# Loading the expert indexes of the first four tiles together, and turning half of the indicators before v is ready, in a one-core Flamingo block

## The chip, the cores and the metric

The kernel runs on one core of a Trainium2 chip. The metric is the device time of one execution in microseconds (us), as the median of several runs. Engines: TensorE (PE; PEld is its weight load), VectorE (DVE), ScalarE (ACT), GpSimd (POOL) and SyncE (SP), which only issues DMAs. Each engine runs its own instructions in the order in which they are written; semaphores tie the engines together.

## The reference

16 batches of 256 tokens with 512 features pass through cross attention and then a mixture of 8 experts, of which each token takes 2.

```python
x = x + tanh(g_xattn[0]) * xattn(layernorm(x), ctx, Wq, Wkv)
x = x + tanh(g_ffn[0]) * ffn(layernorm(x), ...)

def ffn(x, ...):
    probs = softmax(einsum('bsd,de->bse', x, gate_w) + gate_b, axis=1)   # over the tokens of a batch
    vals, idx = top_k(probs, 2)
    h = relu(x @ w1[e] + b1[e]); h = relu(h @ w2[e] + b2[e]); y = relu(h @ w3[e] + b3[e])
    v = einsum('ebso,bse->eo', y, w_tok)      # one row per expert, summed over ALL tokens
    out = einsum('bse,eo->bso', ind, v)       # ind[b,s,e] = 1 where the token takes expert e
```

So the experts' outputs are not given back to their tokens: they are summed into v (8 x 512), and each token adds the two rows of v of its experts.

## The kernel before, in words

Products are made in three passes of split fp32 numbers (hi x hi, hi x lo, lo x hi; lines 1446 to 1448), so nearly every operand has a hi part made by ScalarE and a lo part made by VectorE or GpSimd.

**Attention, batches 0 to 15** (to some 324 us). Each batch is attended, normalised to xn2, sent to DRAM (`xn2_dram`) and gated. The slot of each token in its expert's list is worked out on VectorE (`slots`, lines 1070 to 1094), and GpSimd writes (token, weight) pairs to that slot of `slot_pair` in DRAM with four indirect DMAs per batch (`send_pairs`, line 678). The list of the first 8 tiles is made after 12 batches (`early_table`).

**Expert tiles.** A tile is 352 slots of one expert; tile 0 starts while the last batches are still in work. For a tile m SyncE loads its 352 indexes (`load_idx`, line 535: three DMAs of 128, 128 and 96 pairs, behind a read of the table), GpSimd gathers those rows of xn2 from DRAM into `xg` (`gather`, line 708: three indirect DMAs), and TensorE turns them (`row_transposes`, line 1723). ScalarE and VectorE make et_hi (line 924) and et_lo from the result, TensorE runs layers 1 to 3, and VectorE adds the weighted sum into `v_sum`. From tile 4 on the turning is done by DMAs and VectorE. There is one `idx` and one `xg` buffer: `load_idx(m)` waits for gather m - 1 (semaphore `gathered`), and `gather(m)` waits for index m (`idx_in`) and for `te_done` of tile m - 1.

**Where attention and experts meet,** the order on each engine is written out by hand. On GpSimd: the last batch's part of the loop, `gather(1)`, `send_pairs(13)`, `norm2_scale(15)`, `gather(2)`, `send_pairs(14)`, and so on (lines 728 to 739). `norm2_scale(15)` (lines 645 to 664, output rn) gives the scale with which ScalarE makes xn2 of batch 15 (`norm2`, line 828, xn in the profile); behind it ScalarE has `et_high(1)`, `split_w(0, 1)` (w_hi, line 885) and `gt_high(15)`. VectorE follows with `et_low(1)`, slots(14), `w_low` and `gt_low(15)`. TensorE has the first product of layer 2 of tile 0 (lines 1669 to 1671), `ranks(14)` (line 1517), `xn2_transposes(15)` (line 1460), which waits for xn2 and for the second piece of et_low(1) (its PSUM bank), then the second half of layer 2 and `gate_logits(15)` (line 1565), which waits for gt_low(15). SyncE's order there stands in lines 546 to 568.

**The tail.** After the last tile VectorE makes v in bf16 parts (`v3`, lines 1420 to 1427). TensorE turns the indicators `ind_all` of two batches at a time (`turn_indicators(k)`, k = 0 to 7, four matmuls each, line 1782) into two PSUM banks in turn, and ScalarE copies them to `ind24` (`indicators(k)`, line 973). TensorE turns v (line 1790), VectorE and ScalarE copy it (lines 1429 and 979), and then 32 rows of products follow (line 1803), one per 128 tokens, in 6 banks. VectorE adds 26 of them to x (line 1436), GpSimd 6 (rows 11, 15, ... 31, copied by ScalarE; line 752). SyncE sends a batch of output when its two rows are there (line 619). Groups 2 to 7 of the indicators stand on TensorE ahead of rows 2, 6, 10, 14, 18 and 22.

Of the kernel before, what the change touches and what calls it, by code (L numbers as in the profile page):

```python
# [9 lines left out]
U32 = mybir.dt.uint32  # L10
# [72 lines left out]
EARLY = 8  # L83

# [38 lines left out]
def flamingo_block(nc, x, x_t, ctx_t, g_xattn, g_ffn, wq_t, wk_t, wv, gate_w, gate_b,  # L123
# [15 lines left out]
    with ExitStack() as ctx:  # L139
# [32 lines left out]
        v_sum = alloc(ctx, "v_sum", [P, E, DC], F32)  # L172
        ind_all = alloc(ctx, "ind_all", [P, B, RC, 3, E], BF16)
# [209 lines left out]
        tail_small, wsum_step, part_done = sem("tail_small"), sem("wsum_step"), sem("part_done")  # L383
        v_step, vt_done, v24_ready = sem("v_step"), sem("vt_done"), sem("v24_ready")
# [18 lines left out]
        turn_banks = [bank[2], bank[3]]  # L403
# [32 lines left out]
        def _(sp):  # L436
# [93 lines left out]
            def load_idx(m):  # L530
                need(sp, gathered, 16 * TH * m)
                wait_alone(sp, "sp")
                r = sp.value_load(table[0:1, bass.ds(m, 1), 1:2], min_val=0, max_val=NSLOT - TILE)
                for c, (first, rows) in enumerate(CHUNKS):
                    sp.dma_start(idx[0:rows, c], slot_pair[bass.ds(r + first, rows)]).then_inc(idx_in, 16)
# [13 lines left out]
            load_idx(0)  # L549
# [5 lines left out]
            load_idx(1)  # L555
# [5 lines left out]
            load_idx(2)  # L561
# [6 lines left out]
            load_idx(3)  # L568
# [55 lines left out]
        def _(pool):  # L624
# [70 lines left out]
            def gather(m):  # L695

                need(pool, idx_in, 16 * TH * (m + 1))
# [9 lines left out]
                for c, (_, n) in enumerate(CHUNKS):  # L707
                    pool.indirect_dma_start(xg[0:n, c], None, rows,  # L708
                                            bass.IndirectOffsetOnAxis(ap=idx[0:n, c, 0:1], axis=0)
# [46 lines left out]
        def _(act):  # L756
# [214 lines left out]
            def indicators(k):  # L971
                act.wait_ge(turned, k + 1)
                act.activation(ind24[:, 2 * k * S:2 * (k + 1) * S], turn_banks[k % 2][0:3 * E], ACT.Copy
                               ).then_inc(ind24_done, 1)

            indicators(0)
            indicators(1)
            act.wait_ge(vt_done, 1)
            act.activation(v24[:, D // 2:], bank[1][0:3 * E, 0:D // 2], ACT.Copy).then_inc(v24_ready, 1)
            for n in range(B * RC):  # L980
                if n % 4 == 2 and n // 4 + 2 < PAIRS:
                    indicators(n // 4 + 2)
# [457 lines left out]
        def _(pe):  # L1440
# [335 lines left out]
            def turn_indicators(k):  # L1776
                if k >= 2:
                    pe.wait_ge(ind24_done, k - 1)
                for i in range(2 * RC):
                    rows = ind_all[:, 2 * k + i // RC, i % RC].rearrange("p r e -> p (r e)")  # L1780
                    out = turn_banks[k % 2][0:3 * E, i * P:(i + 1) * P]
# [4 lines left out]
            turn_indicators(0)  # L1786
            turn_indicators(1)
            pe.wait_ge(v_step, 1 + 4)
            for c in range(DC):
                last = pe.matmul(bank[c // 2][0:3 * E, (c % 2) * P:(c % 2 + 1) * P],  # L1790
                                 v3[:, c].rearrange("p r e -> p (r e)"), ident_half[:], start=True, stop=True)
            last.then_inc(vt_done, 1)
            pe.wait_ge(v24_ready, 2)
            for n in range(B * RC):
                if n % 4 == 0:
                    pe.wait_ge(ind24_done, n // 4 + 1)
                if n % 4 == 2 and n // 4 + 2 < PAIRS:
                    turn_indicators(n // 4 + 2)
# [49 lines left out]
```

## Time and profile before

| | |
|---|---|
| median of 3 runs | 922.4 us (921.86 to 922.59) |
| the profiled execution | 923.1 us |
| its span | 921.3 us |
| mean granted clock of TensorE | 0.984 of full speed |
| TensorE busy | 903.1 us, 98% |
| VectorE busy | 710.8 us, 77% |
| ScalarE busy | 506.5 us, 55% |
| GpSimd busy | 284.1 us, 31% |
| DMA | 144.97 MB, mean 157 GB/s |

Times are in us from the start of the span. The span is the profiled execution as the profiler sees it; the execution's own time holds 1.8 us more around it. The clock is given as a share of 2.4 GHz; it has two levels, 1.2 and 2.4 GHz, and a value between them is a mix of both. Matmuls are pipelined: a matmul's start to the start of the next one tells its cost, not its duration. In a timeline the number in square brackets is how long the engine had been idle before the row, and what ended that. An "x3" row holds three instructions without a pause. Releasers are inferred from the last semaphore event before the start.

### The profile page before, as it was taken

The numbers are of one execution on the slowest core, as the hardware profiler recorded it, in microseconds if no ns is written. First come the engines' busy times: TensorE is split into PE (matmuls) and PEld (weight loads), VectorE is DVE, ScalarE is ACT, GpSimd is POOL, SyncE is SP. The second block draws the span as 40 slices with busy tenths as digits, with TensorE's granted clock in tenths as the row PEclk, the third lists the DMA queues.
The fourth block names the chain that finished last, engine by engine and source line by source line (L and its number), as shares of the span: only waits on it lengthen the run. The fifth ranks groups of instructions, "written<-read, shape, count | busy, mean of one in ns | idle before, by whom it ended". The sixth has DMA issues, their size and how long they took to land.

```text
span 921.3 us, 18692 instructions
## 1 busy us (share of the span) xinstructions
PE 903.1 (98%) x5650; PEld 850.8 (92%) x5650; DVE 710.8 (77%) x1305; ACT 506.5 (55%) x703; POOL 284.1 (31%) x314
## 2 busy tenths in 40 slices
PE   9999999999999989999999999999999999999985
PEld 6989888898888889999999999999999999999971
DVE  6667888888888877868777777777777777777665
ACT  5355444554445566556666666666666666666432
POOL 4234555554554458712111111111111111110003
PEclk9999999999999999999999999999999999999995
DMA  7434543345432745377757888853753753751008
GB/s 241 161 122 146 156 149 114 114 161 167 127 92 72 166 125 139 95 172 226 201 156 201 247 245 247 246 157 110 201 156 110 201 156 110 201 156 49 17 31 351
DMA packets 105412, 144.97 MB, mean 157 GB/s; under 512 B 29728, under 2 KB 70432, under 8 KB 102176
## 3 DMA queue, kind: packets, MB, share of 16 engines
q1 hardware_dynamic: 97952, 127.15, 46.2%
q0 software_dynamic: 7424, 17.38, 7.2%
q8 instruction: 18, 0.29, 0.1%
q14 instruction: 18, 0.15, 0.1%
HBM read 112.95 MB, written 31.53 MB: 157 GB/s over the span
## 4 chain that ended last, share of the span: by engine, by line
PE 90%; POOL 2%; issue 2%; DMA 2%; DVE 1%; SPq 1%; ACT 1%; POOLq 0%; DVEq 0%; ACTq 0%
PE bank L1446 28%; PE bank L1448 27%; PE bank L1447 27%; PE bank L1803 1%; POOL slot_pair L678 1%; DMA idx<-slot_pair 1%; PE bank L1567 1%; PE bank L1524 1%; PE bank L1569 0%; PE bank L1586 0%; DMA wk_raw<-in_wk_t 0%; PE bank L1460 0%; PE bank L1480 0%; PE bank L1723 0%; PE bank L1782 0%
## 5 line engine op out<-in xcount | busy, mean ns | idle before, releaser
L1446 PE MATMUL bank<-h_hi,w_hi 128*128 128x352 f32 x744 | 242.2, 326 | 0.0
L1448 PE MATMUL bank<-h_hi,w_lo 128*128 128x352 f32 x744 | 240.7, 324 | 0.0
L1447 PE MATMUL bank<-h_lo,w_hi 128*128 128x352 f32 x744 | 239.7, 322 | 0.0
L708 POOL DMA_INDIRECT xg<-xn_dram,idx x72 | 86.1, 1196 | 367.6 <-DMA idx<-slot_pair 351.9
L1023 DVE TENSOR_TENSOR w_lo<-w_raw,w_hi 128x2048 fp32r<-128x2048 f32 (+1 forms) x74 | 166.6, 2251 | 23.6 <-ACT w_hi L885 18.6
L902 ACT ACTIVATE h<-bank,bias 128x352 f32<-128x352 f32 x192 | 95.9, 551 | 138.3 <-PE bank L1448 137.8
L885 ACT ACTIVATE w_hi<-w_raw 128x2048 fp32r<-128x2048 f32 x71 | 135.5, 1908 | 35.4 <-PE bank L1448 32.0
L1023 DVE TENSOR_TENSOR h_lo<-h,h_hi 128x704 fp32r<-128x704 f32 x88 | 78.1, 888 | 83.0 <-ACT h_hi L908 83.0
L1446 PEld LDWEIGHTS bank<-h_hi,w_hi 128*128 128x128 f32 x744 | 140.5, 189 | 0.0
L1447 PEld LDWEIGHTS bank<-h_lo,w_hi 128*128 128x128 f32 x744 | 140.4, 189 | 0.0
L1448 PEld LDWEIGHTS bank<-h_hi,w_lo 128*128 128x128 f32 x744 | 139.9, 188 | 0.0
L1446 PE MATMUL bank<-et_hi,w_hi 128*128 128x352 f32 x376 | 121.5, 323 | 0.0
L1447 PE MATMUL bank<-et_lo,w_hi 128*128 128x352 f32 x376 | 120.5, 321 | 0.0
L1448 PE MATMUL bank<-et_hi,w_lo 128*128 128x352 f32 x376 | 120.5, 320 | 0.0
L678 POOL DMA_INDIRECT slot_pair<-pair,slot_u x64 | 68.8, 1075 | 68.2 <-DVE pair L1094 47.4
L908 ACT ACTIVATE h_hi<-h 128x704 fp32r<-128x704 f32 x96 | 76.3, 794 | 6.5 <-PE bank L1569 2.7
L1447 PEld LDWEIGHTS bank<-et_lo,w_hi 128*128 128x128 f32 x376 | 70.7, 188 | 0.0
L1446 PEld LDWEIGHTS bank<-et_hi,w_hi 128*128 128x128 f32 x376 | 70.6, 188 | 0.0
L1448 PEld LDWEIGHTS bank<-et_hi,w_lo 128*128 128x128 f32 x376 | 70.5, 188 | 0.0
L1446 PE MATMUL bank<-xt_hi,a_hi 128*128 128x256 f32 x240 | 69.2, 288 | 0.0
L1447 PE MATMUL bank<-xt_lo,a_hi 128*128 128x256 f32 x240 | 67.9, 283 | 0.0
L1448 PE MATMUL bank<-xt_hi,a_lo 128*128 128x256 f32 x240 | 67.9, 283 | 0.0
(222 smaller groups left out, 1740.7 us busy)
## 6 DMA issues: line engine op xcount, KB each, us to landing
w_raw<-in_w SPq DMA_DIRECT2D x24, 1024.0 KB, 5.7
xq<-rows_dram SPq DMA_DIRECT2D x80, 176.0 KB
w_raw<-in_w SPq DMA_DIRECT2D x48, 256.0 KB, 6.9
rows_dram<-xg SPq DMA_DIRECT2D x20, 512.0 KB, 3.3
wb<-slot_pair SPq DMA_DIRECT2D x24, 352.0 KB, 4.4
xt_raw<-in_x_t SPq DMA_DIRECT2D x16, 512.0 KB, 3.8
c_raw<-in_ctx_t SPq DMA_DIRECT2D x16, 512.0 KB, 3.8
x_all<-in_x SPq DMA_DIRECT2D x16, 512.0 KB, 4.8
```

The costliest lines, as they stand in the source:

```text
L678: pool.indirect_dma_start(slot_pair, bass.IndirectOffsetOnAxis(ap=slot_u[:, k, n:n + 1], axis=0), pair[:, k, n], None).then_inc(pair_sent[ ...
L708: pool.indirect_dma_start(xg[0:n, c], None, rows, bass.IndirectOffsetOnAxis(ap=idx[0:n, c, 0:1], axis=0)).then_inc(gathered, 16)
L885: act.activation(w_hi[n][:], w_raw[n][:], ACT.Copy).then_inc(w_his[n], 1)
L902: act.activation(h[:, oc], layer_banks(n, m)[oc][:, 0:TILE], ACT.Relu, bias=bias[n][:, oc:oc + 1]).then_inc(relu_done[n], 1)
L908: act.activation(h_hi[n][:, 2 * k:2 * k + 2], h[:, 2 * k:2 * k + 2], ACT.Copy).then_inc(h_his[n], 1)
L1023: dve.tensor_tensor(dst, src, hi.bitcast(F32), ALU.subtract).then_inc(done, 1)
L1446: pe.matmul(out_ap, lh, rh, start=(i == 0), stop=False)
L1447: pe.matmul(out_ap, lh, rl, start=False, stop=False)
L1448: last = pe.matmul(out_ap, ll, rh, start=False, stop=(i == n - 1))
L1524: last = pe.transpose(bS[:, k * S + c * P:k * S + (c + 1) * P], pexp[:, c, k * P:(k + 1) * P], ident[:])
L1567: pe.matmul(R_LOGIT, gw[:, i, 0:E], gt_lo[:, i], start=False, stop=False)
L1803: pe.matmul(out_banks[n % 6][:], ind24[:, n * P:(n + 1) * P], v24[:], start=True, stop=True).then_inc(o_done, 1)
```

## The change

Indexes: tiles 0 to 3 get an index buffer and a semaphore each (`first_idx`, `first_idx_in`). SyncE loads all four ahead of the first weights, without waiting for a gather; the loads of 1, 2 and 3 go from their old places. Tile 4 uses `idx` first, without a wait for a gather. `gather(m)` waits for the buffer's own semaphore.

Indicators: four PSUM banks hold groups 0 to 3, all turned at the start of the tail; v's transposes then wait for two of ScalarE's copies, since they use banks 0 and 1. Group 4 is turned behind v's transposes, groups 5, 6 and 7 ahead of rows 2, 6 and 10. ScalarE copies groups 4 to 7 in the places of rows 0, 2, 4 and 6.

```diff
+IDX_EARLY = 4
...
+        first_idx = [alloc(ctx, f"first_idx{n}", [P, TH, 2], U32) for n in range(IDX_EARLY)]
...
-        turn_banks = [bank[2], bank[3]]
+        turn_banks = [bank[n] for n in (0, 1, 2, 3, 2, 3, 2, 3)]
...
             def load_idx(m):
-                need(sp, gathered, 16 * TH * m)
-                wait_alone(sp, "sp")
+                if isinstance(m, int) and m < IDX_EARLY:
+                    into, done = first_idx[m], first_idx_in[m]
+                else:
+                    into, done = idx, idx_in
+                    if not (isinstance(m, int) and m == IDX_EARLY):
+                        need(sp, gathered, 16 * TH * m)
+                        wait_alone(sp, "sp")
...
-            load_idx(0)
+            for m in range(IDX_EARLY):
+                load_idx(m)
             sp.wait_ge(qa_done, 2 * B)
             load_w(0, 0)
             load_w(1, 0)
             for n in range(3):
                 load_b(n, 0)
-            load_idx(1)
             store_xn2(B - 2)
...
-            load_idx(2)
...
-            load_idx(3)
...
             def gather(m):
-                need(pool, idx_in, 16 * TH * (m + 1))
+                if isinstance(m, int) and m < IDX_EARLY:
+                    rows_of = first_idx[m]
+                    pool.wait_ge(first_idx_in[m], 16 * TH)
+                else:
+                    rows_of = idx
+                    need(pool, idx_in, 16 * TH * (m - IDX_EARLY + 1))
...
-            indicators(0)
-            indicators(1)
+            for k in range(4):
+                indicators(k)
...
             for n in range(B * RC):
-                if n % 4 == 2 and n // 4 + 2 < PAIRS:
-                    indicators(n // 4 + 2)
+                if n % 2 == 0 and n // 2 + 4 < PAIRS:
+                    indicators(n // 2 + 4)
...
             def turn_indicators(k):
-                if k >= 2:
+                if k >= 4:
                     pe.wait_ge(ind24_done, k - 1)
...
-            turn_indicators(0)
-            turn_indicators(1)
+            for k in range(4):
+                turn_indicators(k)
             pe.wait_ge(v_step, 1 + 4)
+            pe.wait_ge(ind24_done, 2)
...
             last.then_inc(vt_done, 1)
+            turn_indicators(4)
             pe.wait_ge(v24_ready, 2)
...
-                if n % 4 == 2 and n // 4 + 2 < PAIRS:
-                    turn_indicators(n // 4 + 2)
+                if n in (2, 6, 10):
+                    turn_indicators(5 + n // 4)
```

SyncE, from the last index DMA of tile 0 to the first weights, before (L533 and L498 read the table, L508 loads weights):

```order
L535 DMA idx<-slot_pair 96x2
L498 TENSOR_LOAD table
L498 ISA x2
L508 ISA
L508 DMA w_raw<-in_w 32x4x512
```

and with the change, from the last index DMA of tile 2 on (line numbers of the changed kernel, L502 and L512 being the lines of the weights):

```order
L544 DMA first_idx<-slot_pair 96x2
L542 TENSOR_LOAD table
L542 ISA x2
L544 ISA
L544 DMA first_idx<-slot_pair 128x2
L544 ISA
L544 DMA first_idx<-slot_pair 128x2
L544 ISA
L544 DMA first_idx<-slot_pair 96x2
L502 TENSOR_LOAD table
L502 ISA x2
L512 ISA
```

Three such index loads, each with its read of the table, now stand ahead of the first weights.

TensorE in the tail, from the first indicators to the third row, before:

```order
L1782 MATMUL bank<-ident_half,ind_all 24x128 [waits slot_step]
L1782 MATMUL bank<-ident_half,ind_all 24x128 x7
L1790 MATMUL bank<-ident_half,v 24x128 [waits v_step]
L1790 MATMUL bank<-ident_half,v 24x128 x3
L1803 MATMUL bank<-v,ind 128x512 [waits ind24_done,v24_ready]
L1803 MATMUL bank<-v,ind 128x512
L1782 MATMUL bank<-ident_half,ind_all 24x128 [waits ind24_done]
```

and with the change:

```order
L1794 MATMUL bank<-ident_half,ind_all 24x128 [waits slot_step]
L1794 MATMUL bank<-ident_half,ind_all 24x128 x15
L1804 MATMUL bank<-ident_half,v 24x128 [waits ind24_done,v_step]
L1804 MATMUL bank<-ident_half,v 24x128 x3
L1794 MATMUL bank<-ident_half,ind_all 24x128 [waits ind24_done]
L1794 MATMUL bank<-ident_half,ind_all 24x128 x3
L1818 MATMUL bank<-v,ind 128x512 [waits ind24_done,v24_ready]
L1818 MATMUL bank<-v,ind 128x512
L1794 MATMUL bank<-ident_half,ind_all 24x128 [waits ind24_done]
```

Eight more matmuls stand ahead of the transposes of v, four between these and the first row, and v's transposes wait for ScalarE as well.

## Rows read from the trace of the kernel before

**Rows 1.** Waits of TensorE, whole span: engine, line, releaser, us in total, times, longest

```profile
PE bank L1460 <- DVE et_lo L1023: 3.3, 1, 3.3
PE bank L1790 <- DVE v L1427: 2.1, 1, 2.1
```

**Rows 2.** Timeline of TensorE, 319 to 349 us: start, us, engine, line, what, idle before

```profile
319.87 1.58 PE L1723 MATMUL bank<-ident,xg 128*128 128x128 f32 x12
...
334.85 0.41 PE L1669 MATMUL bank<-h_hi,w_hi 128*128 128x352 f32 x1
...
338.75 0.18 PE L1517 MATMUL bank<-ind,tri_half 128*128 128x16 bf16 x1
...
342.22 1.45 PE L1460 MATMUL bank<-ident,xn 128*128 128x128 f32 x8 [3.25 <-DVE et_lo L1023]
343.32 0.64 PE L1446 MATMUL bank<-h_hi,w_hi 128*128 128x352 f32 x1
...
348.64 0.28 PE L1565 MATMUL bank<-gt_hi,gw 128*40 128x256 f32 x1
```

**Rows 3.** Window 340:345: length, busy PE, PEld, DVE, ACT, POOL, PEclk, DMA share, GB/s

```profile
340.00:345.00 5.00, 2.78 (x14) 2.81 (x15) 4.08 (x13) 5.00 (x8) 2.70 (x4) 0.80 0.73 187
```

**Rows 4.** Timeline of GpSimd, 316 to 348 us

```profile
327.23 1.10 POOL L708 DMA_INDIRECT xg<-xn_dram,idx  x1 [10.90 <-DMA idx<-slot_pair]
...
335.79 1.10 POOL L678 DMA_INDIRECT slot_pair<-pair,slot_u  x1 [0.31 <-issue]
...
338.52 0.20 POOL L664 TENSOR_TENSOR rn<-rn 128x2 f32<-128x2 f32 x1
...
347.14 3.07 POOL L678 DMA_INDIRECT slot_pair<-pair,slot_u  x1 [0.30 <-issue]
```

**Rows 5.** Timeline of SyncE's DMA issues, 300 to 315 us

```profile
300.26 1.43 SPq L535 DMA_DIRECT2D idx<-slot_pair  x3
306.30 2.99 SPq L508 DMA_DIRECT2D w_raw<-in_w  x4
...
311.31 2.64 SPq L527 DMA_DIRECT2D bias<-in_b  x3
314.79 1.39 SPq L535 DMA_DIRECT2D idx<-slot_pair  x3
```

**Rows 6.** Timeline of ScalarE, 327 to 342 us

```profile
327.12 1.89 ACT L885 ACTIVATE w_hi<-w_raw 128x2048 fp32r<-128x2048 f32 x1
...
333.30 1.00 ACT L902 ACTIVATE h<-bank,bias 128x352 f32<-128x352 f32 x2 [2.35 <-PE bank L1448]
...
338.75 1.52 ACT L828 ACTIVATE xn<-x_all,rn 128x512 f32<-128x512 f32 x2 [3.63 <-POOL rn L664]
...
341.50 1.91 ACT L885 ACTIVATE w_hi<-w_raw 128x2048 fp32r<-128x2048 f32 x1
```

**Rows 7.** Timeline of VectorE, 331 to 346 us

```profile
331.35 0.25 DVE L1020 BATCH_NORM_AGGREGATE mv<-st 128x2 f32<-128x6 f32 x2
...
340.78 1.75 DVE L1023 TENSOR_TENSOR et_lo<-bank,et_hi 128x512 fp32r<-128x512 f32 x3 [3.60 <-ACT et_hi L924]
...
345.87 1.28 DVE L1023 TENSOR_TENSOR gt_lo<-bank,gt_hi 128x512 fp32r<-128x512 f32 x2
```

**Rows 8.** DMA issues of 310 to 311 us, the last number being us to landing

```profile
w_raw<-in_w SPq DMA_DIRECT2D x1, 1024.0 KB, 13.7
```

**Rows 9.** Timeline of TensorE, VectorE and GpSimd in the tail

```profile
894.03 0.39 PE L1790 MATMUL bank<-ident_half,v 128*24 128x128 bf16 x4 [2.09 <-DVE v L1427]
894.46 0.41 DVE L1429 CAST v<-bank 24x256 bf16<-24x256 f32 x1 [0.48 <-PE bank L1790]
...
902.10 1.29 POOL L752 TENSOR_TENSOR x_all<-v_rows,x_all 128x512 f32<-128x512 f32 x1 [90.15 <-ACT v_rows L986]
```

**Rows 10.** Two windows of the tail, columns as in rows 3

```profile
904.00:905.00 1.00, 1.00 (x6) 0.33 (x4) 0.84 (x3) 0.37 (x1) 0.55 (x1) 0.50 0.73 291
915.00:916.00 1.00, 0.00 (x0) 0.00 (x0) 0.00 (x0) 0.00 (x0) 0.00 (x0) 0.50 1.00 397
```

More of the change, by code:

```diff
@@ L383, in flamingo_block @@
         tail_small, wsum_step, part_done = sem("tail_small"), sem("wsum_step"), sem("part_done")
+        first_idx_in = [sem(f"first_idx_in{n}") for n in range(IDX_EARLY)]
         v_step, vt_done, v24_ready = sem("v_step"), sem("vt_done"), sem("v24_ready")
@@ L530, in load_idx @@
             def load_idx(m):
-                need(sp, gathered, 16 * TH * m)
-                wait_alone(sp, "sp")
+                if isinstance(m, int) and m < IDX_EARLY:
[5 more added lines that the diff above has]
+                        wait_alone(sp, "sp")
                 r = sp.value_load(table[0:1, bass.ds(m, 1), 1:2], min_val=0, max_val=NSLOT - TILE)
                 for c, (first, rows) in enumerate(CHUNKS):
-                    sp.dma_start(idx[0:rows, c], slot_pair[bass.ds(r + first, rows)]).then_inc(idx_in, 16)
+                    sp.dma_start(into[0:rows, c], slot_pair[bass.ds(r + first, rows)]).then_inc(done, 16)
             def load_wb(m):
@@ L708, in gather @@
                     pool.indirect_dma_start(xg[0:n, c], None, rows,
-                                            bass.IndirectOffsetOnAxis(ap=idx[0:n, c, 0:1], axis=0)
+                                            bass.IndirectOffsetOnAxis(ap=rows_of[0:n, c, 0:1], axis=0)
                                             ).then_inc(gathered, 16)
@@ L972, in indicators @@
                 act.wait_ge(turned, k + 1)
-                act.activation(ind24[:, 2 * k * S:2 * (k + 1) * S], turn_banks[k % 2][0:3 * E], ACT.Copy
+                act.activation(ind24[:, 2 * k * S:2 * (k + 1) * S], turn_banks[k][0:3 * E], ACT.Copy
                                ).then_inc(ind24_done, 1)
-            indicators(0)
-            indicators(1)
+            for k in range(4):
+                indicators(k)
             act.wait_ge(vt_done, 1)
@@ L1780, in turn_indicators @@
                     rows = ind_all[:, 2 * k + i // RC, i % RC].rearrange("p r e -> p (r e)")
-                    out = turn_banks[k % 2][0:3 * E, i * P:(i + 1) * P]
+                    out = turn_banks[k][0:3 * E, i * P:(i + 1) * P]
                     last = pe.matmul(out, rows, ident_half[:], start=True, stop=True)
```

## The prediction, written before the changed kernel ran

> **What bounds the kernel now.** I read the waits of TensorE first, then its own timeline, then the chain that released the one wait inside the work, and the tail last. The waits come first because TensorE is busy for 98% of the span (the table above): an edit can pay only where TensorE stands still or is slow, or behind its last product. There are two waits worth naming [rows 1]: 3.3 us before the transposes of the last batch's rows (line 1460), put down to VectorE's et_lo, and 2.1 us before v is transposed (line 1790).
>
> The first one costs more than its 3.25 us [rows 2]. The 24 products of tile 0's second half of layer 2 run from 343.32 to 348.64, 5.32 us. The 24 before the wait, of the same 352 columns, run from 334.85 to 338.75, 3.90 us. The difference of 1.42 us is the clock: 0.80 was granted on average in 340 to 345 us [rows 3], so a part at 1.2 GHz behind the wait, where the stretch before had 2.4 GHz. The place costs 3.25 + 1.42 = 4.67 us.
>
> Who made TensorE wait? Follow it back. GpSimd begins gather(1) at 327.23, after 10.90 us idle for an index DMA [rows 4]. Behind it, in its own order, stand the four sends of batch 13 (the last ends at 336.89) and the small operations that give batch 15's norm its scale (the last ends at 338.72). ScalarE waits 3.63 us for that scale and starts xn at 338.75; et_hi and VectorE's et_lo follow, and TensorE starts at 342.22. The index itself was asked for at 314.79, behind 2 MB of weights and three biases in SyncE's queue [rows 5], while the index of tile 0, asked for at 300.26, met an empty queue. So the index of tile 1 was late by its place in the queue, not by its size.
>
> **The index part of the change.** It moves the index loads of tiles 1, 2 and 3 directly behind that of tile 0, each into a buffer of its own, so none of them needs the gather before it. GpSimd's gather(1) then waits only for the buffer xg, free when TensorE's transposes of tile 0 end (319.87 + 1.58 = 321.45 [rows 2]). I take 321.6 for its start, 5.6 us earlier. The seven DMA issues of gather(1) and the sends took 336.89 - 327.23 = 9.66 us [rows 4], so they end at 331.3. The scale needs batch 15's statistics as well, and the small operations took 338.72 - 336.89 = 1.83 us. ScalarE is free from 338.75 - 3.63 = 335.12 [rows 6], and the statistics end at 331.60 [rows 7]. The scale is there at 331.6 + 1.8 = 333.4, so the late one is now **ScalarE itself, at 335.1**, 3.65 us earlier than before, with 1.7 us to spare for GpSimd. Nothing on ScalarE or VectorE between xn and et_lo waits for anything else, so the piece of et_lo that released TensorE at 342.22 now does so at 338.57. TensorE is ready at 342.22 - 3.25 = 338.97. The wait goes, by a margin of 0.4 us.
>
> What is late next? The gate's logits at 348.64 need gt_lo of batch 15, which ended at 347.15 [rows 7]. It comes behind et_lo and ScalarE's w_hi of 341.50 without a pause, so it moves by the same 3.65, to 343.50. TensorE gets there at 338.97 + 1.10 (the transposes, 342.22 to 343.32) + 3.90 = 343.97. That is 0.5 us of margin; I price it at nothing. From there ScalarE waits for TensorE again, so the later work moves with TensorE.
>
> What the move delays: SyncE issues three more index loads ahead of the weights. One takes 314.79 + 1.39 - 313.95 = 2.23 us with its read of the table [rows 5], so the first weights are issued at about 301.69 + 3 x 2.23 + 0.84 = 309.2 instead of 306.30, 2.9 us later. The weights of layer 2 were issued between 310 and 311 and landed 13.7 us later [rows 8], at 323.7 to 324.7; with all of the delay at 326.6 to 327.6. ScalarE wants them at 327.12 [rows 6]. At worst 0.5 us late, and ScalarE has 2.35 us idle before 333.30 to make it good. At the lower end they are not late at all: gather(0) has the DMA engines to itself meanwhile and is out of the way when the weights come. Cost on the path: 0 between both bounds. The queue's later items (bias, xn2 stores, wb) lose an index load each ahead of them. Load 4 no longer waits for gather(3), but gather(4) is four tiles away from being late: nothing.
>
> **The tail part.** Sixteen indicator transposes instead of eight run while VectorE makes v. TensorE idled 2.09 us there [rows 9], and eight more at some 0.1 us each (0.39 for four of the same kind) take 0.8 of it. The fifth group is issued behind the transposes of v, while VectorE copies v for 0.41 us: 0.39 beside 0.41, nothing. The new wait for two copies of ScalarE ends before v is made. The first output row starts where it did. Between rows, three groups of four fewer stand on TensorE, 3 x 0.39 = 1.2 us. I give none of it to the sum: after all engines were done, in 915 to 916 us, the DMA engines still had a share of 1.00 and moved 397 GB/s [rows 10]. The outputs are 16 x 512 KB = 8.39 MB, 21 us at that rate, more than the 20 us from the end of the copy of v (894.87) to a time at which no engine works any more, so **the output queue sets the end**, and it starts with batch 0, which does not move. What can be won is the hole of 904 to 905, where the share was 0.73, some 0.3 us: there batch 5 waited for GpSimd's first row (902.10 to 903.39 [rows 9]). The groups between rows ahead of that row are as many as before, so I expect it to stay. Bounds of this part: 0 to -0.3, and +0.1 if the fifth group outlasts the copy.
>
> **Sum.** -3.25 - 1.42 + 0 = -4.67 us. Of the profiled execution, 923.1 becomes 918.4 and its span 921.3 becomes 916.6. The median of the runs, 922.4, is 0.7 below that execution; the same -4.67 on it gives **917.7 us**.
>
> **Rivals.**
> (A) *GpSimd's issues grow slow.* gather(1) moves under VectorE's weight subtractions, and one issue of this kind took 3.07 us at 347.14 instead of 1.1 [rows 4]. One such is 2.0 us, against 1.7 of margin; two are 4.0, and xn then starts at 337.4, TensorE at 340.9. Of the 3.25 us, 1.3 are won and the clock may fall all the same: gain 1.3 to 2.8, time 919.6 to 921.1. For it: such issues are in the trace. Against: 9.66 us already hold issues beside VectorE.
> (B) *The tail's clock stays up.* In 904 to 905 us TensorE was busy all the time at a granted 0.50, 1.2 GHz. The idle ahead of the rows shrinks from 2.1 to 1.3 us; if that keeps the 2.4 GHz, GpSimd's first row comes earlier and the hole closes: 917.4. Against: ten us into the rows a TensorE without a pause still had not got its clock back. The Trainium skill, "TensorE: Matmul & The Clock Gate", under "What's actually happening", has sustained activity release the throttle; by that rule rows in succession would run at full clock. This trace does not agree for rows of 24 partitions.
> (C) *The weights become the wait* (slower). If nine small transfers hold up the queue for more than their issues, layer 2's weights come late. From their landing, w_hi 1.89, relu 1.00 [rows 6] and two splits of 704 columns have to pass before TensorE's 334.85. I estimate the splits from the w_hi row (2048 columns in 1.89) and the gt_lo row (1024 in 1.28) at 0.7 + 0.9. So landings up to 330.3 cost nothing, some 6 us later than before, and only 10.7 us later is the gain eaten. At 14 us the time is 922.4 + 3.3 = 925.7. Against: the queue is empty when they go out, and 2.9 us is all that their issues take.
> (D) *The change does not free gather(1)*, because another wait stands behind the index: 922.4. Against: te_done is 5.8 us older than the start, and the buffer is free.
>
> **Chances.** Forecast 0.70; A 0.13; B 0.10; C 0.04; D 0.03. A measurement of this kernel tells about 0.2%, 1.8 us, from no change. Faster: forecast, B and most of A, 0.91. Within: D and the slowest of A, 0.05. Slower: C, 0.04. The range runs from 916.7 (B, and 0.7 us between runs as 921.86 to 922.59 shows) to 919.9 (the better end of A), which leaves out some 0.15.
>
> **What would show it.** Right: gather(1) starts at about 321.6 with no wait for an index; xn begins at 335.1 with no wait for rn; no idle before the transposes of line 1460's last call; the granted clock is 1.00 in 340 to 345; tile 0's 24 products take 3.9 us. The tail from the transposes of v to the end of the span keeps its 921.3 - 894.03 = 27.3 us, with a DMA share near 1.00 to the end. Wrong: xn still waits for rn (A); w_hi of layer 2 waits for a DMA (C); the tail is shorter by more than 0.3 us, so that production and not the output queue bounds it.

## The result, and the profile after

| | before | changed |
|---|---|---|
| median, first measurement (3 runs each) | 922.4 us (921.86 to 922.59) | 916.73 us (916.5 to 917.42) |
| ratio to before | | 0.9938 [0.9925, 0.9952] |
| ratio, measured again (7 runs, 27 of before) | | 0.9961 [0.9946, 0.9976] |
| ratio, a third time (6 runs, 17 of before) | | 0.9956 [0.9944, 0.9968] |
| profiled execution, its span | 923.1, 921.3 us | 916.73, 914.5 us |
| mean granted clock | 0.984 | 0.988 |

The changed kernel is faster, as forecast, but 5.7 us faster in the first measurement where 4.7 was forecast. Two more measurements, with more runs, gave 3.6 and 4.1 us (1 - 0.9961 and 1 - 0.9956 of 921.6; the medians themselves lie 3.6 and 3.0 us apart). The forecast lies between these three figures, and for a wrong reason, as the experiments show: one term of its sum was too large, and another, which was put at nothing, was worth 1.1 to 1.7 us.

The waits of TensorE in the changed kernel, columns as in [rows 1]:

```profile
PE bank L1804 <- DVE v L1439: 1.6, 1, 1.6
PE bank L1482 <- POOL zeros L632: 1.2, 1, 1.2
PE bank L1472 <- ACT xn L840: 0.9, 2, 0.6
```

The 3.3 us of [rows 1] ahead of batch 15's transposes are gone (line 1472 is the old 1460; none of its 0.9 lies ahead of batch 15's transposes, where the timeline below shows no idle time), and the wait for v has shrunk from 2.1 to 1.6. GpSimd's timeline, as [rows 4]:

```profile
322.61 1.10 POOL L720 DMA_INDIRECT xg<-xn_dram,first_idx  x1 [5.97 <-issue]
...
331.01 0.97 POOL L685 DMA_INDIRECT slot_pair<-pair,slot_u  x1 [0.30 <-issue]
332.07 0.97 POOL L652 TENSOR_SCALAR rn<-mv 128x2 f32<-128x2 f32 x1
333.12 1.22 POOL L654 TENSOR_TENSOR rn<-rn,mhalf 128x2 f32<-128x2 f32 x1
334.54 0.43 POOL L669 TENSOR_SCALAR rn<-mv 128x2 f32<-128x2 f32 x1 [0.20 <-POOL rn L654]
335.06 0.20 POOL L671 TENSOR_TENSOR rn<-rn 128x2 f32<-128x2 f32 x1
```

gather(1) waits for no index. It begins at 322.61, 4.6 us earlier than in [rows 4], not the 5.6 forecast (tile 0's transposes ended at 321.76, and 0.85 us lie between that and the gather's start, where the forecast had 0.15), and the small operations behind the sends took 3.2 us instead of 1.8. The scale was ready at 335.26 and not at 333.4. ScalarE, which answers to [rows 6]:

```profile
334.64 0.79 ACT L920 ACTIVATE h_hi<-h 128x704 fp32r<-128x704 f32 x1
335.34 1.51 ACT L840 ACTIVATE xn<-x_all,rn 128x512 f32<-128x512 f32 x2
```

xn begins without a wait, at 335.34 (forecast 335.1). The 1.7 us that GpSimd was to have in hand had gone to almost nothing. TensorE, the last operation ahead of the transposes, these, and what follows, as in [rows 2]:

```profile
338.73 0.17 PE L1530 MATMUL bank<-ind,ones_half 128*128 128x16 bf16 x1
338.83 1.21 PE L1472 MATMUL bank<-ident,xn 128*128 128x128 f32 x8
339.79 0.41 PE L1458 MATMUL bank<-h_hi,w_hi 128*128 128x352 f32 x1
...
343.82 0.31 PE L1577 MATMUL bank<-gt_hi,gw 128*40 128x256 f32 x1
```

```profile
340.00:345.00 5.00, 5.00 (x35) 4.61 (x34) 4.96 (x8) 3.66 (x6) 3.47 (x2) 1.00 0.58 198
```

No idle time, the clock at 1.00 in the window of [rows 3], and the gate's product at 343.82 instead of 348.64: 4.8 us. At v's transposes it is 894.03 - 889.37 = 4.66 us, the 4.67 of the sum. But the spans differ by 6.8, so another 2.1 us were won in the tail. SyncE, to compare with [rows 5], had the weights out at 310.40 (forecast 309.2), and no w_hi waited for them:

```profile
300.42 9.10 SPq L544 DMA_DIRECT2D first_idx<-slot_pair  x12
310.40 2.98 SPq L512 DMA_DIRECT2D w_raw<-in_w  x4
```

The tail of the changed kernel: v's transposes, GpSimd's first and last row, as in [rows 9], then a window, as in [rows 10]:

```profile
889.37 0.39 PE L1804 MATMUL bank<-ident_half,v 128*24 128x128 bf16 x4 [1.65 <-DVE v L1439]
...
896.52 1.27 POOL L764 TENSOR_TENSOR x_all<-v_rows,x_all 128x512 f32<-128x512 f32 x1 [89.26 <-ACT v_rows L998]
...
905.46 1.28 POOL L764 TENSOR_TENSOR x_all<-v_rows,x_all 128x512 f32<-128x512 f32 x1 [0.52 <-ACT v_rows L998]
```

```profile
900.00:901.00 1.00, 1.00 (x3) 0.10 (x1) 1.00 (x3) 0.00 (x1) 0.92 (x1) 0.50 0.99 393
```

GpSimd's first row comes 7.15 us behind v's transposes, 8.07 before, and the hole in the transfers is gone in this execution. What ended the tail was not plain yet.

### The profile page after: what moved, and what is told of

It reads as the page before. It is cut to its first block, busy times and chain, and to the rows that moved or that the text cites. A ratio compares the mean times of both kernels' runs of the same rounds, so it can differ in the third digit from the quotient of the medians.

```text
span 914.5 us, 18688 instructions
## 1 busy us (share of the span) xinstructions
PE 899.8 (98%) x5650; PEld 848.2 (93%) x5650; DVE 711.4 (78%) x1305; ACT 506.3 (55%) x703; POOL 286.9 (31%) x314
## 4 chain that ended last, share of the span: by engine, by line
PE 94%; POOL 1%; DVE 1%; issue 1%; ACT 0%; DMA 0%; POOLq 0%; SPq 0%; DVEq 0%
PE bank L1458 29%; PE bank L1459 28%; PE bank L1460 28%; PE bank L1818 1%; POOL slot_pair L685 1%; PE bank L1579 1%; PE bank L1536 1%; PE bank L1735 1%; PE bank L1581 1%; PE bank L1598 1%; PE bank L1472 0%; DMA wk_raw<-in_wk_t 0%; PE bank L1492 0%; PE bank L1493 0%; PE bank L1487 0%
## 5 line engine op out<-in xcount | busy, mean ns | idle before, releaser
L720 POOL DMA_INDIRECT xg<-xn_dram,idx x60 | 72.2, 1203 | 352.8 <-DMA idx<-slot_pair 340.5
```

Of the source, the lines that this page charges most:

```text
L720: pool.indirect_dma_start(xg[0:n, c], None, rows, bass.IndirectOffsetOnAxis(ap=rows_of[0:n, c, 0:1], axis=0)).then_inc(gathered, 16)
```

## The experiments

The later runs form four groups, each on one chip with the kernel before beside the others (its median 921.5, 921.6, 921.2 and 921.6 us); a ratio is always to the kernel before of the same group. Microseconds of gain are worked out from the ratios; the differences of the medians lie up to 1.1 us from them. For the profiles I cut the span at two places that every kernel has: A, from the first product of layer 2 of tile 0 to v's transposes (boundary and expert tiles), and T, from there to the end (tail). Before: A 894.03 - 334.85 = 559.2, T 27.3. Changed: 554.6 and 25.1.

### The two parts alone

The index part alone (the change without its indicator part), twice; the second time beside the whole change:

> The index part of the change alone, on the tail of before. Theory 1 (the wait of 3.25 us and the slow clock behind it are worth 4.7 us, and the tail gave about 1.0 of the 5.7): this gains 4.7, ratio 0.9949. Theory 2 (all of the gain comes from the index part, the tail is bound by the output queue and gives nothing): 5.7, ratio 0.9938.

> The index part alone, again, now beside the whole change. If the profile that was late from its start-up (first weights 1.2 us late) was an accident: v's transposes begin at 889.5 to 890.5, as in the whole change. Theory that the parts add: 1 to 2 us above the whole change and 1 to 2 us below before. Rival that the index part is all of it: the same as the whole change within 0.3 us.

The indicator part alone, also twice:

> The indicator part alone, with the index loads of before. Theory 1: it gains 1.0 us, ratio 0.9989; in the trace the clock falls later after the first row, GpSimd's first row comes earlier and the hole in the output queue is closed. Theory 2: 0 (-0.3 to +0.1), ratio 1.000. The profile tells whether the last DMA engine still runs 1.2 us longer than the others, as it did in the profile of before.

> The indicator part alone, again. Theory that the parts add: 1 to 2 us above the whole change, 1 to 2 us below before. Theory that the boundary's wait is worth 4.7 us by itself: 4.5 us above the whole change and the same as before. In its profile the wait of TensorE ahead of the transposes of xn2 of batch 15 should be there again, 1.5 to 3.3 us.

The whole change again:

> The changed kernel again, beside the two parts alone and before. Theory (the first comparison is the kernels' own): 4 to 6 us below before, both parts' gains adding (the parts alone measured -1.0 and -1.7 us against before on another occasion, which would leave 1 to 3 us that only the pair gives). Rival (the profiled execution of before at the first measurement was one of its longer ones: wait of 3.3 us and a fall of the clock at the boundary, and a DMA engine that ran on alone at the end): 2.5 to 3.5 us below before, the sum of the parts. Its profile: no wait ahead of the transposes of xn2 of batch 15, clock 1.00 between 335 and 350, v's transposes to the end 25.0 to 25.5.

Measured in the group of these three: index part 0.9980 [0.9968, 0.9992], indicator part 0.9982 [0.9971, 0.9994], both 0.9961 [0.9946, 0.9976]. The first time the parts alone gave 0.9987 [0.9976, 0.9998] and 0.9988 [0.9976, 0.9999]. So **the parts add**, within intervals of some 0.12% to either side: 0.20% and 0.18% against 0.39%. The indicator part, priced at nothing, is worth about as much as the index part, priced at everything. The rival of the last expectation, that the first profile of before was a long one, fits best (2.5 to 3.5 us there, 3.6 measured).

In the profiles of the index part A was 554.6 both times and T 26.7 and 27.5, the old tail. In those of the indicator part A was 558.3 and 556.0, T 26.3 and 25.2. Waits of TensorE with the indicator part alone (its first profile):

```profile
PE bank L1460 <- DVE et_lo L1023: 1.5, 1, 1.5
...
PE bank L1669 <- DVE h_lo L1023: 1.1, 1, 1.1
```

The boundary's wait is back, half as long as in [rows 1], with another of 1.1 us ahead of it, and the granted clock in 340 to 345 stayed at 1.00.

### What the boundary costs

Filler on TensorE in the kernel before, ahead of the transposes that waited:

```diff
             ranks(B - 2)
+            for n in range(48):
+                pe.matmul(bank[2][:, 0:P], ident_half[:], ones_half[:], start=True, stop=True)
             xn2_transposes(B - 1)
```

> Before with 48 matmuls of 128 columns on constants, written to a free bank ahead of the transposes that wait. They take some 2.7 us and end before the wait does, so the wait's end does not move. If the 1.42 us behind the wait are the clock that fell while TensorE stood idle, the clock stays at 1.00 in 340 to 345 us and the gain is 1.4 us, ratio 0.9985. If they are something else (the products waiting for data), 0.

Measured: 1.0017 [1.0005, 1.0029], 1.6 us slower, A 558.6. The filler did not do what was meant. It ran from 340.00 to 342.84, and the transposes followed at 343.04; in the indicator part's profile they began 1.44 us behind the start of VectorE's et_lo, which here would be 341.7 (et_lo began at 340.23). So the filler ended behind the wait and held TensorE some 1.4 us by itself. The clock stayed at 1.00, but it did so in most profiles with the old boundary (below), so this run does not price the clock.

The scale of batch 15 ahead of the sends of batch 13 on GpSimd, in the kernel before:

```diff
             gather(1)
-            send_pairs(B - 3, (B - 3) % 2)
             norm2_scale(B - 1)
+            send_pairs(B - 3, (B - 3) % 2)
```

> Before with one edit in GpSimd's order: the scale of batch 15 is made ahead of the four sends of batch 13. gather(1) stays as late as before, 327.2 us. If the chain to TensorE's wait is gather(1), sends, scale, xn, et_lo, as predicted, the scale is there by 333.6, xn starts at 335.1 when ScalarE is free, and the gain is that of the index part, 4.7 us. If gather(1)'s data, not the scale, is what counts, nothing is gained.

Measured: 1.0049 [1.0029, 1.0068], slower. TensorE's waits:

```profile
PE bank L1446 <- ACT h L902: 2.9, 1, 2.9
...
PE bank L1723 <- DMA xg<-xn_dram,idx: 2.0, 1, 2.0
```

The wait at line 1460 is gone, as meant, and two others took its place behind it: at 355.6 TensorE had waited 2.0 us for the rows of gather(2), which began at 342.20 instead of 339.33, and at 360.2 it had waited 2.9 us for ScalarE's h; the granted clock was 0.50 from 358 to 364. Moving the wait's last link alone makes the kernel slower. The expectation had gather(1) at 327.2 in this kernel; it came at 325.39.

The kernel before once more:

> The kernel before, profiled a second time. The stretch from layer 2 of tile 0 to v's transposes took 559.2 us in its first profile, and 556.1 to 558.3 in three kernels with the same boundary. Theory (a part of the boundary's wait, and the fall of the clock behind it, come in some executions only): 556 to 558.5 us, no fall of the clock or a shorter wait than 3.3 us. Rival (they belong to this kernel): 559 us, wait 3.3 us, clock at 1.2 GHz behind it. In both, GpSimd's last row plus its 8.6 us of drain ends the program, 27.3 us behind v's transposes.

Its second profile had A 554.8, as short as with the change, T 26.9, and no wait for et_lo at all. GpSimd's gather(1) and TensorE:

```profile
323.97 1.10 POOL L708 DMA_INDIRECT xg<-xn_dram,idx  x1 [6.84 <-DMA idx<-slot_pair]
```

```profile
340.07 1.21 PE L1460 MATMUL bank<-ident,xn 128*128 128x128 f32 x8
```

The first theory's signs are there, no fall of the clock and no wait, but A lies below its 556 to 558.5: the same instructions in the same order, and gather(1), released by the index, came 3.3 us earlier although the index was asked for 2.2 us later (316.98, against 314.79 in [rows 5]). Median of the timed runs: 921.25, ratio 0.9995 [0.9984, 1.0007], as it should be.

The four own buffers, but the loads of the indexes 1, 2 and 3 at their old places:

```diff
-            for m in range(IDX_EARLY):
+            for m in range(1):
                 load_idx(m)
...
                 load_b(n, 0)
+            load_idx(1)
...
             load_w(0, 1)
+            load_idx(2)
...
             load_w(0, 2)
+            load_idx(3)
```

> The changed kernel, with the four buffers of its own, but the indexes of tiles 1, 2 and 3 loaded at their old places, behind the weights and biases. Theory (what held the second gather was the place in the queue, behind 3 MB of weights, and not the one shared buffer): that gather waits for its index to about 327 us again, and the stretch from layer 2 of tile 0 to v's transposes takes 556 to 559 us instead of 554.6; the time is 1.5 to 2 us above the changed kernel in this call. Rival (the shared buffer's wait for the first gather was it): the gather at 322.6 us, 554.6 us, and the time of the changed kernel.

Its gather(1), ScalarE's second pair of h (layer 1 of tile 0) and xn, and two waits of TensorE:

```profile
325.94 2.13 POOL L723 DMA_INDIRECT xg<-xn_dram,first_idx  x1 [8.32 <-DMA first_idx<-slot_pair]
```

```profile
336.29 1.00 ACT L917 ACTIVATE h<-bank,bias 128x352 f32<-128x352 f32 x2 [3.95 <-remote]
...
339.15 1.52 ACT L843 ACTIVATE xn<-x_all,rn 128x512 f32<-128x512 f32 x2 [1.04 <-POOL rn L674]
```

```profile
PE bank L1475 <- DVE et_lo L1038: 1.2, 1, 1.2
PE bank L1684 <- DVE h_lo L1038: 1.2, 1, 1.2
```

A was 557.5. gather(1) waits for its index although no buffer is shared any more, so the place in the queue (behind 2 MB of weights; the 3 MB of the expectation is a slip) is enough to make the index late. The time was 0.9961 [0.9945, 0.9976] against 0.9956 [0.9944, 0.9968] for the changed kernel, 0.3 us, where 1.5 to 2 were expected: six runs each neither show that cost nor exclude it.

Of the two waits only the one for et_lo hangs on gather(1) by the chain of the prediction (sends, rn, xn, et_lo). The one for h_lo hangs on ScalarE's h, which had been idle for 3.95 us where the profile of before shows 2.35, and was released by what the profile calls "remote". **A second path of the boundary** shows here that the prediction did not have. This idle time was 3.8 to 5.1 us in five of the eight profiles with the index loads at their old places (indicator part twice, filler, old places, and the kernel with VectorE's rows, below), and 1.8 to 2.4 in the other three and in all ten with an early index. (For the second of the indicator part the profile names TensorE's product as the releaser, as before.) In two of the five (the second of the indicator part, and VectorE's rows) xn did not wait for rn at all: their loss is that of h alone. What makes h late, and whether the late index has a part in it, no run shows.

Only tiles 0 and 1 ahead of the weights, the other two behind the biases:

```diff
-            for m in range(IDX_EARLY):
+            for m in range(2):
                 load_idx(m)
...
             store_xn2(B - 2)
+            load_idx(2)
+            load_idx(3)
```

> The changed kernel, but only the indexes of tiles 0 and 1 are loaded ahead of the first weights; those of tiles 2 and 3 follow behind the biases. Theory (the index part gives its gain through the second gather alone, and gives 0.7 to 0.9 us back before the boundary, since the first product of layer 2 of tile 0 began at 335.9 us in eight traces with early indexes and at 335.0 in five without, because the weights are issued 3 to 4 us later): 0.4 to 0.9 us faster than the changed kernel in this call, layer 2 of tile 0 at 335.0 and v's transposes 554.6 us behind it, as in the changed kernel. Rival (the later weights cost nothing and the 0.9 us is chance): the same within 0.3 us.

> The changed kernel, for comparison with the three others on one chip: 3.2 to 4.2 us below before, 554.6 us from layer 2 of tile 0 to v's transposes.

Measured 0.9957 [0.9945, 0.997] and 0.9956 [0.9944, 0.9968]: the same. The weights went out at 306.57 instead of 309.57 and layer 2 began at 334.9 instead of 335.9, but in the second profile of before it began at 336.0 as well, and in the first of the changed kernel, with its weights at 310.40, at 334.8: that difference is not the weights'. The early indexes of tiles 2 and 3 add nothing that can be measured, so the index part lies in that of tile 1, and the later weights cost nothing that can be measured, as forecast.

gather(1)'s start and A, all profiles with the old boundary and neither the filler nor the norm first: 323.97 and 554.8 (before, second), 324.94 and 558.3 (indicator part), 325.65 and 556.0 (the same again), 325.94 and 557.5 (old places), 326.42 and 558.3 (the kernel with VectorE's rows, below), 327.23 and 559.2 (before, first). With the early index: 554.5 to 554.7 in ten profiles. The six average 557.4, 2.8 us above; the timed runs, which are many more, put the index part at 1.2 and 1.8 us. The first profile of before, on which the forecast stands, was the extreme of the six. The clock fell behind the boundary in two of them: there, and in the kernel with VectorE's rows, where one wait of 2.1 us for h_lo stood alone and the window 340 to 345 had 0.66. Where TensorE stood 1.0 to 1.5 us at a time it stayed at 1.00.

### What ends the tail

The output a row earlier, on top of the change (batch 0 as two DMAs):

```diff
-            for b in range(B):
+            for n in range(RC):
+                sp.wait_ge(res_dve, dve_rows(n + 1))
+                sp.dma_start(out_v[0][:, n], x_all[:, 0, n]).then_inc(out_sent, 16)
+            for b in range(1, B):
```

> The changed kernel with batch 0 of the output sent as two DMAs, one for each row, so that the first transfer begins a row earlier. Theory (the output queue moves at 400 GB/s without a pause from its first transfer to its last and sets the end): 0.3 to 0.6 us faster than the whole change in this call, since the first row is ready about 0.6 us ahead of the second. Rival (the rows' production or the last landing sets the end): within 0.1 us of it.

Measured 0.9963 [0.995, 0.9977] beside 0.9961 for the change: nothing. In its profile the first transfer did go out earlier, but the queue then stood idle for longer (its share was 0.78 in 895 to 896 and 0.55 in 900 to 901), so the first transfer alone does not set the end. That sent me to the last instructions of the program. The rows of the line that closes it, in the profile of the index part alone (old tail, second profile; columns: line, queue, what, count, ns min/median/max, start):

```profile
L141 POOLq DRAIN  x1: 8585/8585/8585, 908.7 to 908.7; - x1
L141 SPq DRAIN  x1: 7/7/7, 915.4 to 915.4; - x1
```

**GpSimd's drain takes 8.6 us.** It begins with GpSimd's last row (908.77, 1.26 us long), so it ends 7.3 us behind it: at 917.33. SyncE had seen its last output land at 915.26, the span ends at 917.55. In this execution GpSimd's last row ends the program and the output queue has 2 us in hand. The same rows of the changed kernel (first profile):

```profile
L141 POOLq DRAIN  x1: 8602/8602/8602, 905.4 to 905.4; - x1
L141 SPq DRAIN  x1: 7/7/7, 914.3 to 914.3; - x1
```

Here GpSimd is through at 905.4 + 8.6 = 914.0 and SyncE at 914.3: the two stand level. And of the kernel before:

```profile
L139 POOLq DRAIN  x1: 8585/8585/8585, 912.5 to 912.5; - x1
L139 SPq COMPARE_BRANCH  x1: 38/38/38, 920.5 to 920.5; - x1
```

912.5 + 8.6 = 921.1, 0.2 before the end of its span. In this execution the output was late as well (a few packets still ran at 29 GB/s in 919 to 920), which is why both looked level. So it was in the second profile of before:

```profile
L139 POOLq DRAIN  x1: 8618/8618/8618, 908.8 to 908.8; - x1
L139 SPq DRAIN  x1: 13/13/13, 917.1 to 917.1; - x1
```

Counted from v's transposes in all profiles, GpSimd is through at 26.4 to 28.1 us in the six with the old tail and at 24.6 to 25.4 in the eight with the new one. The last output lands at 24.8 to 26.5 and at 24.7 to 26.1: **the landing did not move with the change, GpSimd did**. In the old tail GpSimd was the later of the two each time (by 0.5 to 2.1 us), in the new one the output was later, or level within 0.2 us. (SyncE's closing branch, COMPARE_BRANCH, is taken for the landing.) The landings spread over 1.8 us for the same transfers; in some profiles a few packets ran on by themselves at the end, as above, and why is not shown.

What delays GpSimd's last row is seen in the chain that ended last. Old tail, index part alone, second profile (start, us, engine, line; L1794 are turned indicators, L1815 rows):

```profile
896.11 0.53 PE bank L1794 x4
896.64 1.81 PE bank L1815 x4
...
903.68 2.68 PE bank L1815 x6
906.39 0.61 ACT v_rows L998
907.07 1.26 POOL x_all L764
908.74 1.30 POOLq L141
```

and in the changed kernel:

```profile
894.32 0.53 PE bank L1794 x4
894.85 8.12 PE bank L1818 x18
902.99 0.60 ACT v_rows L998
903.67 1.27 POOL x_all L764
904.94 0.48 issue
905.42 1.31 POOLq L141
```

Every group of indicators between rows is 0.53 us at 1.2 GHz (0.33 at 2.4) of a chain that ends with GpSimd. Six stand between rows in the old tail and three with the change; at the price of 0.53 there are five and one in these two profiles. GpSimd's drain begins 16.0 us behind v's transposes instead of 18.6, but not all of these 2.6 us are the order's: the clock fell 3.0 us behind v's transposes here and 1.7 in the other. In the second profile of the changed kernel it fell at 1.7 as well, and there the drain begins at 16.7. So the order is worth 1.9 us at the same clock, 3 x 0.53 = 1.6 of it the three groups, and the later fall another 0.7. Then the theory was tested from both sides. GpSimd's rows to VectorE, in the kernel before:

```diff
         def by_pool(n):
-            return n >= 8 and n % 4 == 3
+            return False
```

> The kernel before, but VectorE adds all 32 rows of the tail, so that GpSimd (and its drain of 8.6 us, which in every trace so far begins at GpSimd's last row) has nothing there. New theory of the tail: in the kernel before, GpSimd's last row plus its drain ends the program, 1.9 us behind the last landing of the output; in the changed one the two end together. Expected: 1.5 to 2.2 us faster than before, v's transposes to the end 25.1 to 25.5 instead of 27.3, and the last landing to the end 0.4 instead of 2.3. Theory of the prediction (the output queue sets the end): 0 to 0.4 us faster. Rival (VectorE at 0.6 us a row is too slow alone): 0.5 us or more slower.

Two more additions behind GpSimd's last row, in the changed kernel:

```diff
             for n in filter(by_pool, range(B * RC)):
...
+            for n in range(2):
+                pool.tensor_tensor(pool_pad[:, n], v_rows[:, 1], v_rows[:, 1], ALU.add)
```

> The changed kernel with two more additions of 1.3 us each on GpSimd behind its last row, into a buffer that nobody reads. New theory (GpSimd's last work plus 8.6 us of drain is a floor of the end, and stands level with the output's last landing): 2.1 to 2.6 us slower than the changed kernel, v's transposes to the end about 27.7, drain again 8.6 us long. Theory that the output queue sets the end: no difference, since the last row is added over 5 us before the last landing.

The kernel with the two additions, its GpSimd and its closing rows:

```profile
906.52 1.29 POOL L765 TENSOR_TENSOR x_all<-v_rows,x_all 128x512 f32<-128x512 f32 x1 [0.52 <-ACT v_rows L1001]
907.76 2.04 POOL L767 TENSOR_TENSOR pool_pad<-v_rows 128x512 f32<-128x512 f32 x2
```

```profile
L141 POOLq DRAIN  x1: 10583/10583/10583, 906.5 to 906.5; - x1
L141 SPq COMPARE_BRANCH  x1: 38/38/38, 915.2 to 915.2; - x1
```

The output had landed at 915.2, and the program went on to 917.3. The drain was 10.6 us long, not 8.6 as I expected: it holds the work still queued, here 1.3 + 2.0 us, and again 7.3 behind it. T was 26.9, the time 0.9985 [0.9974, 0.9995] against 0.9961 and 0.9956 without the additions in other groups, 2.2 and 2.7 us slower (expected 2.1 to 2.6, although the two additions took 1.0 each and not 1.3). The changed kernel did not run in this group; beside the two kernels of the group without GpSimd's rows (below) it is 0.8 and 1.1 us slower. **Shown** by the trace: work on GpSimd that nobody reads, done 5 us before the last output landed, holds the end of the program 2 us behind that landing. That it costs about its own length in the median rests on the comparison between groups.

The kernel before with all rows on VectorE had T 25.8 (expected 25.1 to 25.5), and its closing rows are

```profile
L139 POOLq DRAIN  x1: 10820/10820/10820, 807.7 to 807.7; - x1
L139 SPq DRAIN  x1: 13/13/13, 918.8 to 918.8; - x1
```

with the drain 100 us before the end and the span's end at 919.1, 0.4 behind the last landing. The time was 0.9987 [0.9975, 0.9999], 1.2 us, under the 1.5 to 2.2 expected (the medians differ by 0.7 only): what lies outside the span was at least 2.1 us in its runs and at least 1.7 in those of before, so some of it came back behind the last instruction. Why, I did not find.

The same on top of the change, alone and with the two DMAs for batch 0:

> The same in the changed kernel. New theory: GpSimd's drain and the output queue end within 0.4 us of each other there, so only the hole in the transfers goes: 0.1 to 0.6 us faster than the changed kernel (918.0 in the last call), and 1.5 to 4 us faster than the previous kernel of this call, which is what the index part is worth by itself once the tails are the same. Rival (the indicators' place matters in another way than by GpSimd's last row): the difference of these two kernels is over 4 us.

> The changed kernel with all rows by VectorE and the first batch of the output sent as two DMAs of a row each. The last call's kernel with the two DMAs alone gained nothing, since the queue then ran dry for longer ahead of GpSimd's first row. Theory: with no such row there, the earlier start is kept, 0.3 to 0.7 us faster than the kernel without it in this call. Rival (a pair of rows takes about as long to make as to send, so the queue runs dry again): within 0.2 us.

Measured 0.9971 [0.996, 0.9982] and 0.9966 [0.9954, 0.9977]. Against the 0.9961 and 0.9956 of the changed kernel in other groups these are no gain; the 0.1 to 0.6 us expected of the first did not come, and the two DMAs on top, for which 0.3 to 0.7 were expected, are not separated from it (0.05%). The first is 1.5 us faster than the kernel before with the same rows on VectorE (0.9971 against 0.9987, same group), at the lower end of the 1.5 to 4 expected for the index part with the tails alike. The first had T 25.1 (the changed kernel 25.1 to 26.5), the second 26.5: in both GpSimd was out of the way and only the output queue was left. No version that I ran beats the changed kernel by what can be measured.

Mean of T: old order of the indicators with GpSimd's rows, five profiles (before twice, index part twice, filler), 27.1 us (the kernel with the norm first had 28.3; its clock fell before v's transposes); new order, eight profiles with GpSimd's six rows and nothing behind them, 25.6. The difference, 1.5 us, fits the 1.1 and 1.7 us of the indicator part alone.

## Why the prediction was right and wrong

- **"The index of tile 1 was late by its place in the queue."** Right; own buffers at the old places left gather(1) at 325.94 with 8.32 us of waiting. How late is another matter (third point).
- **The chain from gather(1) to TensorE, and its arithmetic.** Right in its links: no wait for rn, none for et_lo, clock 1.00, 24 products in 4.0 us, and 4.66 us won at v's transposes for 4.67 forecast. But gather(1) came 1.0 us later than forecast and GpSimd's small operations took 1.4 us longer. The margin of 1.7 us was all but used up; a little more and rival A would have held. And the boundary has a second path, ScalarE's late h, which made TensorE wait 1.0 to 2.1 us in five profiles and is not in the prediction at all.
- **"The place costs 3.25 + 1.42 = 4.67 us."** One of the two steps that failed, by its size: it is the sum's only term, and the runs put the part at 1.2 and 1.8 us. It was read from one execution, and the place is not a constant. By A it cost 4.6 us there, 0.2 in the second profile of the same kernel, where the index landed earlier for no reason that a run shows, and 1.4 to 3.7 in the four others. The fall of the clock that made up 1.42 of it appeared in two of six profiles with the old boundary.
- **The later weights at nothing.** Right in what can be seen: w_hi waited for no DMA, and the kernel with the weights 3.0 us earlier took the same time. Rival C did not appear.
- **"The output queue sets the end", and with it the tail at 0 with bounds of 0 to -0.3.** Wrong, and this is the other step that failed, by its mechanism: the part measured 1.1 and 1.7 us alone, and 2.1 in the first pair of profiles. The window of 915 to 916 us in [rows 10] showed busy DMA engines and idle compute engines, and I took what is busy last for what ends last. The old tail ended with GpSimd's drain, 0.5 to 2.1 us behind the last landing. That the output's landing does not move was right (24.7 to 26.5 us behind v's transposes in both orders); it was not the end. The 1.2 us on TensorE between the rows (1.6 at the 1.2 GHz that the tail had) were seen, and given away.
- **Rival B.** The clock did not stay up: 0.50 in the window 900 to 901, with TensorE busy all of it. But the hole and GpSimd's first row did go with the clock, as it says, in both orders. In the six profiles with GpSimd's rows in which it fell 1.6 to 1.9 us behind v's transposes, the first row came at 8.1 to 8.3 us and the hole was there, with a DMA share of 0.55 to 0.73 in a window of 1 us. Where it fell at 2.2 us or later, eight profiles, the row came at 6.7 to 7.8 and there was no hole. The changed kernel had both kinds, and so had the old tail. That the order leaves the first row where it was is what the prediction said; most of the gain, at the last row, came without the clock.

So a sum of one term came near by luck, through two errors of opposite sign: 4.7 for the index part that gives 1.2 to 1.8 on the median, and 0 for an indicator part that gives as much. What the first measurement has above the others (5.7 against 3.6 and 4.1 us) is not explained by a step: it had three runs of each kernel, and the kernel before ranges over 4 to 5 us (918.75 to 923.45 in one group). Open too are why two index DMAs of the same kernel land 3 us apart, what makes ScalarE's h late, and why the last landing moves by up to 1.8 us; no run was made for these.

## What to carry to other kernels

Before a tail is put down to a transfer, look at the last instructions of every engine, the drains too: the end is the later of the last landing and each engine's last work plus its drain, and an engine with a long drain should get its last work early or none. And a wait that hangs on a DMA's landing is not a constant: take a second profile of the unchanged kernel before its length goes into a sum, because one execution can hold all of it and the next almost nothing.

## What the runs showed of the hardware that was not expected

- GpSimd's drain at the program's end lasts 7.3 us behind its last addition (8.585 us with one queued, 10.583 with three: begun with the last of the kernel's rows, it holds the queued work), while VectorE's row lasts 1.2 to 2.9 us with its queued work in it, ScalarE's 0.6 and SyncE's 0.01. Where GpSimd was through 100 us earlier it lasted 10.8 and held up nothing at the end of the span. I had no row for it: the chain of before ends with it under the name POOLq, and shows 1.30 us of it.
- A small index DMA (1 KB) behind 2 MB of weights: gather(1), which waits for it, began 7.0 us after its issue in one execution and 12.4 us in another of the same kernel.
- GpSimd's small operations grow long beside VectorE's work on weights: the same two operations on 128x2 elements took 0.97 and 1.22 us at 332.07, and 0.23 and 0.73 at 336.90 in the kernel with the old places, where VectorE stood idle for 2.2 us. Two issues of a send in the same stretch as VectorE's w_lo of 128x2048 (2.3 us long) took 2.23 and 3.07 us instead of 0.97, at 341.22 and 343.76 in the changed kernel and at 344.60 and 347.14 before.
- In the tail TensorE ran at 1.2 GHz from the fall of the clock to its last row in every profile; in that of before it was busy 1.00 of each window from 896 to 911 us, at a granted 0.50. The Trainium skill, "TensorE: Matmul & The Clock Gate", under "What's actually happening", has sustained activity release the throttle; no trace here shows that for the tail's rows, whose operands have 24 partitions.
